# Masked linear gated by a LoRA layer: new orders for the first products and for a build of weights

## Chip, cores and metric

The kernel runs on one core of one Trainium2 chip. The metric is device time in microseconds for one execution. The engines are TensorE (PE in the profile, with PEld for its weight loads), VectorE (DVE), ScalarE (ACT), GpSimd (POOL) and SyncE (SP), which here issues every DMA.

## What is computed

The reference, cut to what matters (x is 2 x 1024 x 1024 in f32, all matrices are 1024 x 1024, the mask is one of 32 x 32 blocks, 8 experts have rank 64):

```python
xn = (x - mean(x)) / sqrt(var(x) + 1e-5)             # over the last axis
bm = mask.reshape(32, 32, 32, 32).sum(axis=(1, 3)) > 0
w  = weight with every 32 x 32 block multiplied by bm
s  = einsum('bsk,nk->bsn', xn, w) + bias
q  = einsum('bi,ki->bk', xn.mean(axis=1), Wq)
coeffs = softmax(einsum('bk,ek->be', q, lora_keys) / sqrt(128))
base  = einsum('bsi,oi->bso', xn, W_org)
h     = einsum('bsi,eir->bser', xn, lora_down)
delta = einsum('be,bser,ero->bso', coeffs, h, lora_up)
out = x + s * silu(base + delta)
```

## The kernel before

**Tiling.** The 2048 rows of x are 16 tiles of 128 rows, two tiles to a group. Groups 0 to 7 multiply all rows by the masked weight (the first matrix, giving s). Groups 8 to 11 and 12 to 15 take the rows of batch 0 and of batch 1 again, now with the second matrix, W_org plus the LoRA part mixed with the batch's coefficients. So the second matrix is built twice, once for each batch; the first build stands between products P58 and P59 (191 to 230 us).

**Products.** PE does all of it in numbered products P0 to P114, most of them four k-chunks of 512 columns (`products()`). f32 operands are split into a high and a low part of type fp32r, and a chunk is three matmuls: high by high, high by low, low by high (lines L1011 to L1013 of `triple`). Groups 0 to 2 are "plain": eight products each, one for every choice of row tile, half of the columns and half of k. P0 to P3 (row tiles 0 and 1, first half of the columns) are not split at all and run as f32 (L1110, `whole`); P4 is row tile 2, P5 row tile 3. From group 3 on, seven products on sums of blocks take the place of eight. Steps E0.c.p are the same kind of product for the first build: part of up by part of down, for column block c and the p-th of the seven.

**What a plain product needs.** A tile of x is loaded (LX), gets its statistics on DVE (SN: L1326 to L1330) and its rstd on POOL (SR), is normalized in two halves (LN: L1335 on DVE, L1552 on POOL), transposed on PE in two halves of four transposes (TX, L1048) and copied out of PSUM by ACT (TC, L1164). The mask comes in four quarters (LM). Each has two counts of 1024 columns (CA: on DVE L1340, on ACT L1198), a compare (CB, DVE, L1347, which writes bmx), a small matmul that spreads it over the partitions (CP, PE, L1040), a copy to SBUF (CM, DVE, L1355) and the multiplications with the weight pieces (W: DVE L1360, POOL L1566). Splits of rows are steps H (ACT, L1221) and V (DVE, L1394); splits of matrices are HB (ACT, L1235) and VB (DVE, L1394); those for the build are U and VU.

**Warm-up.** Before any of it, PE does 29 transposes of an identity matrix (`WARM`, L1030) into an accumulator that nobody reads.

**What sets the order.** Everything is written out by hand. `ORDER` holds five strings, one for each of SP, PE, ACT, DVE and POOL, and each word is one step that the engine takes in that order (`order_of`). Each engine waits on semaphores for what a step needs, so a step that waits holds up all that stand behind it on its engine. SP issues all DMAs in one queue in this way: loads of x (LX, later LT and LG for transposed tiles), masks (LM), weights (LW), keys and Wq (LY, LK), the build's parts of up (LU), of the split down matrix (LD, L943, into b_hi and d_snaps) and of W_org (LE, L958), s and x for the last sums (LB, LR), and stores of xn (RS) and of s (ST). In PSUM there are six accumulators (psA) and two banks for everything small (psM); a step that takes a bank waits until the one before it in that bank has been read.

## Time and profile before

| | us |
|---|---|
| median of the runs shown (429.3, 431.19, 430.07) | 430.07 |
| profiled execution, its own time | 429.73 |
| its span | 427.9 |

| engine | busy us | share of the span |
|---|---|---|
| PE | 414.2 | 97% |
| PEld (weight loads, beside PE) | 336.1 | 79% |
| DVE | 382.6 | 89% |
| ACT | 240.8 | 56% |
| POOL | 52.7 | 12% |

HBM moved 257 GB/s over the span, and the mean granted clock of TensorE was 0.991 of full speed. How to read it: PE's busy times are ends of pipelined matmuls, so that matmuls overlap in the table of busy times, and what PE is doing is read from the distance between two starts. The idle time before an instruction and what ended it stand in brackets in a timeline; engines that are not the bound may idle at no cost. A row of a table of stretches gives the stretch and its length, then the busy time and the number of instructions of each engine (PE, PEld, DVE, ACT, POOL; fewer where the view is cut down to some), then the granted clock as a share of 2.4 GHz, the busy share of the DMA engines and GB/s. Rows that carry the argument stand in a section of their own below.

### The profile page before, as it was taken

The numbers are of one execution on the slowest core, as the hardware profiler recorded it, in microseconds if no ns is written. First come the engines' busy times: TensorE is split into PE (matmuls) and PEld (weight loads), VectorE is DVE, ScalarE is ACT, GpSimd is POOL, SyncE is SP. The second block draws the span as 40 slices with busy tenths as digits, with TensorE's granted clock in tenths as the row PEclk, the third lists the DMA queues.
The fourth block names the chain that finished last, engine by engine and source line by source line (L and its number), as shares of the span: only waits on it lengthen the run. The fifth ranks groups of instructions, "written<-read, shape, count | busy, mean of one in ns | idle before, by whom it ended". The sixth has DMA issues, their size and how long they took to land.

```text
span 427.9 us, 6112 instructions
## 1 busy us (share of the span) xinstructions
PE 414.2 (97%) x1857; PEld 336.1 (79%) x1857; DVE 382.6 (89%) x592; ACT 240.8 (56%) x427; POOL 52.7 (12%) x61
## 2 busy tenths in 40 slices
PE   6699999999999999999999999999999999999995
PEld 6357888888888888877887888887788888888885
DVE  5789989999899999799999989889899999997556
ACT  3385459879835525495457555445754584634412
POOL 4221302321220010000212010100002110001100
PEclk9699999999999999999999999999999999999999
DMA  8994448878688884999997135599899933367674
GB/s 299 408 409 185 125 146 303 312 225 288 221 306 313 300 289 163 364 379 303 295 382 268 61 123 196 170 369 360 295 368 371 352 100 124 94 227 236 189 249 162
DMA packets 45280, 110.51 MB, mean 258 GB/s; under 512 B 4928, under 2 KB 6208, under 8 KB 44480
## 3 DMA queue, kind: packets, MB, share of 16 engines
q1 hardware_dynamic: 45248, 110.12, 73.0%
q8 instruction: 15, 0.25, 0.2%
q14 instruction: 17, 0.14, 0.1%
HBM read 77.60 MB, written 32.51 MB: 257 GB/s over the span
## 4 chain that ended last, share of the span: by engine, by line
PE 36%; DMA 6%; DVE 6%; issue 4%; ACT 2%; SPq 1%; DVEq 0%; ACTq 0%
PE psA L1011 12%; PE psA L1012 12%; PE psA L1013 12%; DMA b_hi<-d_dram 2%; DMA d_snaps<-d_dram 1%; DMA b_raw<-in_up_dram 1%; DMA s_in<-s_dram 1%; DMA xres<-in_x_nat_dram 1%; DVE cst L1509 1%; DVE a_lo L1394 1%; DVE b_lo L1394 1%; DVE b_raw L1404 1%; SPq L974 0%; DVE cst L1477 0%; ACT cst L1295 0%
## 5 line engine op out<-in xcount | busy, mean ns | idle before, releaser
L1011 PE MATMUL psA<-b_hi,a_hi 128*128 128x512 f32 (+1 forms) x444 | 173.4, 391 | 0.6 <-ACT snaps L1279 0.6
L1013 PE MATMUL psA<-b_hi,a_lo 128*128 128x512 f32 (+1 forms) x444 | 172.1, 388 | 0.0
L1012 PE MATMUL psA<-b_lo,a_hi 128*128 128x512 f32 (+1 forms) x444 | 172.0, 387 | 0.0
L1011 PEld LDWEIGHTS psA<-b_hi,a_hi 128*128 128x128 f32 x444 | 83.4, 188 | 18.4 <-ACT snaps L1279 1.3
L1013 PEld LDWEIGHTS psA<-b_hi,a_lo 128*128 128x128 f32 x444 | 83.4, 188 | 17.3
L1012 PEld LDWEIGHTS psA<-b_lo,a_hi 128*128 128x128 f32 x444 | 83.4, 188 | 16.4
L1394 DVE TENSOR_TENSOR b_lo<-b_raw,b_hi 128x512 fp32r<-128x512 f32 (+2 forms) x78 | 59.6, 790 | 0.2 <-ACT b_hi L1235 0.2
L1235 ACT ACTIVATE b_hi<-b_raw 128x512 fp32r<-128x512 f32 (+2 forms) x66 | 44.7, 716 | 20.4 <-DVE b_raw L1401 5.1
L1279 ACT ACTIVATE snaps<-psA 128x512 f32<-128x512 f32 x39 | 23.1, 591 | 39.6 <-PE psA L1013 39.6
L1221 ACT ACTIVATE a_hi<-s_raw 128x512 fp32r<-128x512 f32 x52 | 31.7, 623 | 15.3 <-DVE s_raw L1385 13.6
L1394 DVE TENSOR_TENSOR a_lo<-s_raw,a_hi 128x512 fp32r<-128x512 f32 x52 | 35.1, 689 | 1.0 <-ACT a_hi L1221 0.8
L1221 ACT ACTIVATE a_hi<-xq 128x512 fp32r<-128x512 f32 x43 | 26.2, 622 | 13.4 <-PE psA L1013 8.2
L1394 DVE TENSOR_TENSOR a_lo<-xq,a_hi 128x512 fp32r<-128x512 f32 x43 | 29.2, 686 | 2.5 <-ACT a_hi L1221 2.5
L1509 DVE TENSOR_TENSOR cst<-cst,s_in 128x512 f32<-128x512 f32 x31 | 21.3, 688 | 9.0 <-DMA s_in<-s_dram 4.9
L1477 DVE TENSOR_TENSOR cst<-psA,snaps 128x512 f32<-128x512 f32 x37 | 25.2, 686 | 2.0 <-issue 1.3
L1011 PE MATMUL psA<-b_hi 128*128 128x512 f32 x64 | 25.0, 390 | 0.9 <-DMA b_hi<-d_dram 0.9
L1012 PE MATMUL psA<-b_lo,b_hi 128*128 128x512 f32 x64 | 24.9, 389 | 0.0
L1013 PE MATMUL psA<-b_hi 128*128 128x512 f32 x64 | 24.9, 389 | 0.0
L1515 DVE TENSOR_TENSOR cst<-cst,xres 128x512 f32<-128x512 f32 x30 | 20.5, 688 | 4.7 <-DMA xres<-in_x_nat_dram 4.0
L1295 ACT ACTIVATE cst<-cst 128x512 f32<-128x512 f32 x23 | 14.4, 626 | 13.6 <-DVE cst L1477 12.6
L1374 DVE TENSOR_REDUCE xpart<-xq 128x8 f32<-128x1024 f32 x16 | 19.2, 1212 | 0.0
L1110 PE MATMUL psA<-b_raw,xq 128*128 128x512 f32 x32 | 17.3, 696 | 1.6 <-POOL b_raw L1566 1.6
(143 smaller groups left out, 557.8 us busy)
## 6 DMA issues: line engine op xcount, KB each, us to landing
b_hi<-d_dram SPq DMA_DIRECT2D x24, 512.0 KB, 5.8
xn_dram<-xq SPq DMA_DIRECT2D x16, 512.0 KB, 5.4
s_dram<-cst SPq DMA_DIRECT2D x32, 256.0 KB, 5.2
xq<-xn_dram SPq DMA_DIRECT2D x16, 512.0 KB, 5.2
worg_sb<-in_w_org_dram SPq DMA_DIRECT2D x32, 256.0 KB, 4.9
s_in<-s_dram SPq DMA_DIRECT2D x32, 256.0 KB, 4.2
xres<-in_x_nat_dram SPq DMA_DIRECT2D x32, 256.0 KB, 4.3
out_dram<-cst SPq DMA_DIRECT2D x31, 256.0 KB, 4.0
```

What stands on the lines that cost most here:

```text
L1011: nc.tensor.matmul(ps, l_hi, r_hi, start=first, stop=False, skip_group_check=True)
L1012: nc.tensor.matmul(ps, l_hi, r_lo, start=False, stop=False, skip_group_check=True)
L1013: return nc.tensor.matmul(ps, l_lo, r_hi, start=False, stop=over, skip_group_check=True)
L1110: ins = nc.tensor.matmul(bank, a_quarter(0, i[0], i[2])[:, c * P:(c + 1) * P], w_raw(W_OPS.index(op))[:, c, :], start=c == 0 and first, st ...
L1221: nc.scalar.activation(a_hi[:, m % ARING, :], a_source(m), ACT.Copy).then_inc(act_hi, 1)
L1235: nc.scalar.activation(b_hi[:, hi_of.get(op, op), b_piece(s, op, pc), :], b_source(s, op, pc), ACT.Copy)\
L1279: nc.scalar.activation(snap(n), bank_of(n), ACT.Copy).then_inc(act_post, 1)
L1374: nc.vector.tensor_reduce(xpart[:, t, :], x_tile(t // 2, t % 2).rearrange("p (k r) -> p k r", r=P), AX.X, ALU.add).then_inc(dve_R, 1)
L1394: nc.vector.tensor_tensor(lo, raw, hi.bitcast(F32), ALU.subtract).then_inc(dve_lo, 1)
L1477: nc.vector.tensor_tensor(cst_of(n), bank, snap(copied), ALU.add).then_inc(dve_post, 1)
L1509: nc.vector.tensor_tensor(cst_of(n), cst_of(n), s_in[:, j % 4, :], ALU.mult).then_inc(dve_post, 1)
L1515: nc.vector.tensor_tensor(cst_of(n), cst_of(n), xres[:, j % 4, :], ALU.add).then_inc(dve_res, 1)
```

## The change

Only the table of orders changes, and a new kind of step is added to PE's list. F k.n is n idle transposes of the identity, as in the warm-up, into the same accumulator; PE's list has F0.10 and F1.8 behind the two halves of TX0. The first lines of PE's order, and the new branch:

```diff
-    TX0.0 TX0.1 CP0 P0 TX1.0 TX1.1 CP1 TX2.0 TX2.1 P1 P2 CP2 TX3.0 P3 TX3.1 K P4 CP3 TX4.0 P5 TX4.1 P6 P7 P8 P9 P10
+    CP0 TX0.0 TX0.1 F0.10 F1.8 CP1 TX2.0 TX2.1 P0 TX1.0 TX1.1 P1 P2 CP2 P3 TX3.0 P4 TX3.1 P5 K CP3 P6 TX4.0 P7 TX4.1 P8
...
-                if kind == "CP":
+                if kind == "F":
+                    for _ in range(st[2]):
+                        nc.tensor.matmul(psA[:, ACC - 1, 0:P], ident[:, :], ident[:, :], start=True, stop=True,
+                                         is_transpose=True)
+                elif kind == "CP":
```

The other lists change as follows.

- SP: the second mask and the first two pieces of weights now stand ahead of x 1 and x 3, and the keys and some weights come earlier; the stores of xn and s of the first 60 us are in another order. In the build, two parts of d, two of W_org and three stores change places.
- ACT: begins with three mask counts (one of mask 0, both of mask 1), and takes the second count of mask 3 from DVE; its splits of the first matrix's pieces and its copies of x stand in another order.
- DVE: gives away that count; multiplies weight piece 0 of the first quarter in place of piece 3; compares mask 0 right behind its count. In the build it takes two low splits and a sum in another order.
- POOL: rstd of x 2 ahead of that of x 0, and weight piece 3 in place of piece 0.

The matrices, the tiles and the arithmetic are those of before. In the changed kernel the table of orders is three lines shorter and the new branch adds four, so lines ahead of the branch have a number lower by three (L1011 is L1008, L1030 L1027) and lines behind it one higher by one (L1048 is L1049, L1110 L1111, L1394 L1395).

PE's list from its first step on, before (L1040 is CP, L1048 the transposes of x, L1110 the products P0 to P3; `x_nat_sb` holds tiles 0 and 1, `x_nat` later ones):

```order
L1030 MATMUL psA<-ident 128x128 x29
L1048 MATMUL psA<-ident,x_nat_sb 128x128 x8
L1040 MATMUL psM<-bmx,sel 128x16 x4
L1110 MATMUL psA<-b_raw,xq 128x512 x4
L1048 MATMUL psA<-ident,x_nat_sb 128x128 x8
L1040 MATMUL psM<-bmx,sel 128x16 x4
L1048 MATMUL psM<-ident,x_nat_61 128x128 x8
L1110 MATMUL psA<-b_raw,xq 128x512 x8
```

PE's list now:

```order
L1027 MATMUL psA<-ident 128x128 x29
L1041 MATMUL psM<-bmx,sel 128x16 x4
L1049 MATMUL psA<-ident,x_nat_sb 128x128 x8
L1033 MATMUL psA<-ident 128x128 x18
L1041 MATMUL psM<-bmx,sel 128x16 x4
L1049 MATMUL psM<-ident,x_nat_61 128x128 x8
L1111 MATMUL psA<-b_raw,xq 128x512 x4
L1049 MATMUL psA<-ident,x_nat_sb 128x128 x8
L1111 MATMUL psA<-b_raw,xq 128x512 x8
```

CP0 stands ahead of tile 0's transposes instead of behind them, the 18 idle transposes are new, and CP1 and the transposes of tile 2 moved from behind P0 to ahead of it.

DVE's list behind the statistics of x tiles 0 and 2, before, from mask 0's count (L1340) to the multiplications of the weights (L1360):

```order
L1340 TENSOR_REDUCE cnt<-masks 128x1
L1326 BN_STATS nat_stats<-x_nat_sb 128x6 x2
L1328 BN_AGGR nat_mv<-nat_stats 128x2
L1329 TENSOR_SCALAR stat<-nat_mv 128x1
L1330 TENSOR_SCALAR var<-nat_mv 128x1
L1347 SCALAR_TENSOR_TENSOR bmx<-cnt,diag 128x16
L1355 COPY bmask<-psM 128x64
L1326 BN_STATS nat_stats<-x_nat_61 128x6 x2
L1328 BN_AGGR nat_mv<-nat_stats 128x2
L1329 TENSOR_SCALAR stat<-nat_mv 128x1
L1330 TENSOR_SCALAR var<-nat_mv 128x1
L1360 TENSOR_TENSOR b_raw<-b_raw,bmask 128x512 x3
```

DVE's list at the same place now, from mask 0's count (L1341) on:

```order
L1341 TENSOR_REDUCE cnt<-masks 128x1
L1348 SCALAR_TENSOR_TENSOR bmx<-cnt,diag 128x16
L1336 TENSOR_SCALAR x_nat_sb<-x_nat_sb,stat 128x512
L1356 COPY bmask<-psM 128x64
L1336 TENSOR_SCALAR x_nat_61<-x_nat_61,stat 128x512 x2
L1361 TENSOR_TENSOR b_raw<-b_raw,bmask 128x512 x2
L1348 SCALAR_TENSOR_TENSOR bmx<-cnt,diag 128x16
L1361 TENSOR_TENSOR b_raw<-b_raw,bmask 128x512
L1356 COPY bmask<-psM 128x64
```

The compare (`bmx`) follows the count at once, half of tile 0 is normalized behind it and not ahead of the count, and the statistics of tiles 1 and 3 have moved behind the multiplications.

DVE's list in the first build, where the low splits of up's sums (`a_lo<-a_raw,a_hi`) are made, before, from 190 us on:

```order
L1414 TENSOR_TENSOR b_raw_51<-a_raw_55,b_raw_51 128x512
L1394 TENSOR_TENSOR a_lo_54<-a_raw_55,a_hi_53 128x512 x3
L1394 TENSOR_TENSOR b_lo_50<-b_raw_51,b_hi_49 128x512
L1414 TENSOR_TENSOR temp_62<-a_raw_55,b_raw_51 128x512
L1477 TENSOR_TENSOR cst_60<-psA,snaps_58 128x512
L1394 TENSOR_TENSOR a_lo_54<-a_raw_55,a_hi_53 128x512
L1394 TENSOR_TENSOR b_lo_50<-b_raw_51,b_hi_49 128x512
```

DVE's list at the same place now:

```order
L1415 TENSOR_TENSOR b_raw_51<-a_raw_55,b_raw_51 128x512
L1395 TENSOR_TENSOR a_lo_54<-a_raw_55,a_hi_53 128x512 x3
L1415 TENSOR_TENSOR temp_62<-a_raw_55,b_raw_51 128x512
L1395 TENSOR_TENSOR a_lo_54<-a_raw_55,a_hi_53 128x512
L1395 TENSOR_TENSOR b_lo_50<-b_raw_51,b_hi_49 128x512 x2
L1410 TENSOR_TENSOR b_raw_51<-b_raw_51,worg_sb_67 128x512
L1395 TENSOR_TENSOR a_lo_54<-a_raw_55,a_hi_53 128x512
L1395 TENSOR_TENSOR b_lo_50<-b_raw_51,b_hi_49 128x512
L1478 TENSOR_TENSOR cst_60<-psA,snaps_58 128x512
```

The low split that follows the three in a row stood behind a `b_lo` and a `cst` (the sum for s of block 56) and now stands ahead of both.

SP's list in the first build, from the loads of s at 217.7 us on, before (`d_snaps` is the part of d that the last products of the build take, `worg_sb` is W_org):

```order
L974 DMA s_in_70<-s_dram 128x512 x2
L958 DMA worg_sb_67<-in_w_org_dram 128x512 x4
L915 DMA xn_dram<-xq_56 128x1024
L974 DMA s_in_70<-s_dram 128x512
L943 DMA d_snaps_59<-d7_dram 128x512
L910 DMA xq_56<-xn_dram 128x1024
L958 DMA worg_sb_67<-in_w_org_dram 128x512
```

SP's list around the last load of `d_snaps` now:

```order
L955 DMA worg_sb_67<-in_w_org_dram 128x512
L940 DMA d_snaps_59<-d7_dram 128x512
L955 DMA worg_sb_67<-in_w_org_dram 128x512 x2
L940 DMA d_snaps_59<-d7_dram 128x512
L990 DMA s_dram<-cst_60 128x512
L955 DMA worg_sb_67<-in_w_org_dram 128x512 x2
L990 DMA s_dram<-cst_60 128x512
L907 DMA xq_56<-xn_dram 128x1024
```

The last `d_snaps` stood behind four loads of W_org in a row, a store of xn and loads of s; it now stands ahead of the last two loads of W_org and of those.

## Rows read from the trace of the kernel before

**Rows 1.** The page's first line.

```profile
span 427.9 us, 6112 instructions
```

**Rows 2.** Timeline of PE, first 40 us: start us, us, instruction [idle before <-releaser].

```profile
1.57 5.93 PE L1030 MATMUL psA<-ident 128*128 128x128 f32 x29 [1.57 <-POOL ident L1528]
8.04 1.09 PE L1048 MATMUL psA<-ident,x_nat_sb 128*128 128x128 f32 x8 [0.55 <-DVE x_nat_sb L1335]
...
14.45 6.66 PE L1110 MATMUL psA<-b_raw,xq 128*128 128x512 f32 x8 [1.59 <-POOL b_raw L1566]
...
22.88 7.03 PE L1110 MATMUL psA<-b_raw,xq 128*128 128x512 f32 x16
...
35.98 0.48 PE L1011 MATMUL psA<-b_hi,a_hi 128*128 128x512 f32 x1
```

**Rows 3.** Busy time by engine in stretches, with the granted TensorE clock (PEclk).

```profile
9.20:13.60 4.40, 0.24 (x4) 0.18 (x4) 3.72 (x9) 2.79 (x6) 0.89 (x2) 1.00 1.00 401
13.60:14.40 0.80, 0.00 (x0) 0.00 (x0) 0.77 (x3) 0.00 (x0) 0.80 (x2) 0.53 1.01 420
...
17.10:20.40 3.30, 3.30 (x5) 1.33 (x4) 1.84 (x5) 1.99 (x4) 0.00 (x0) 0.50 1.05 406
...
20.60:23.00 2.40, 2.40 (x23) 2.03 (x22) 0.90 (x3) 0.60 (x1) 0.59 (x1) 1.00 1.03 434
```

**Rows 4.** The same view, the warm-up transposes (L1030) alone.

```profile
1.50:4.20 2.70, 2.63 (x13) 2.63 (x14) 1.00 0.88 311
...
6.80:7.50 0.70, 0.69 (x6) 0.46 (x4) 1.00 0.95 375
```

**Rows 5.** The same view, PE alone, at the end of the span.

```profile
423.60:426.60 3.00, 0.00 (x0) 1.00 0.40 143
426.70:427.80 1.10, 0.00 (x0) 0.50 0.16 53
```

**Rows 6.** Timeline of DVE, 4 to 27 us: a mask count, three mask multiplications.

```profile
9.32 1.22 DVE L1340 TENSOR_REDUCE cnt<-masks 128x1 f32<-128x1024 int32 x1 [1.34 <-DMA masks<-in_mask_dram]
...
14.72 2.07 DVE L1360 TENSOR_TENSOR b_raw<-b_raw,bmask 128x512 f32<-128x512 f32 x3
```

**Rows 7.** Timeline of ACT, 8 to 26 us: copy of x, mask count, split.

```profile
8.73 0.60 ACT L1164 ACTIVATE xq<-psA 128x512 f32<-128x512 f32 x1 [6.67 <-PE psA L1048]
9.32 1.06 ACT L1198 ACTIVATE masks<-masks 128x1024 f32<-128x1024 int32 x1
...
16.23 0.63 ACT L1235 ACTIVATE b_hi<-b_raw 128x512 fp32r<-128x512 f32 x1 [4.24 <-DVE b_raw L1360]
```

**Rows 8.** The first load of weights (line L899): issue and landing.

```profile
L899 SPq DMA_DIRECT2D b_raw<-in_weight_dram x1: 446/446/446, 3.1 to 3.1; - x1
...
DMA to landing us min/median/max: 10.0/10.0/10.0
```

**Rows 9.** Timeline of PE in the first build, two places.

```profile
194.26 0.39 PE L1012 MATMUL psA<-a_lo,b_hi 128*128 128x512 f32 x1
194.48 0.39 PE L1013 MATMUL psA<-a_hi,b_hi 128*128 128x512 f32 x1
195.09 0.50 PE L1011 MATMUL psA<-a_hi,b_hi 128*128 128x512 f32 x1 [0.22 <-DVE a_lo L1394]
195.43 0.40 PE L1012 MATMUL psA<-a_lo,b_hi 128*128 128x512 f32 x1
...
228.35 0.39 PE L1013 MATMUL psA<-a_hi,d_snaps 128*128 128x512 f32 x1
228.96 0.47 PE L1011 MATMUL psA<-a_hi,d_snaps 128*128 128x512 f32 x1 [0.22 <-DMA d_snaps<-d_dram]
```

**Rows 10.** Timeline of DVE in the first build.

```profile
194.35 0.69 DVE L1394 TENSOR_TENSOR a_lo<-a_raw,a_hi 128x512 fp32r<-128x512 f32 x1
```

**Rows 11.** Timeline of SyncE in the first build: DMA issues.

```profile
218.58 3.55 SPq L958 DMA_DIRECT2D worg_sb<-in_w_org_dram  x4
...
223.26 1.27 SPq L943 DMA_DIRECT2D d_snaps<-d_dram  x1
```

143 lines of the change are left out of this document (70 added, 73 removed).

## The prediction

> **What bounds the kernel now.** I read the page first, then the timeline of TensorE (PE) over the first 40 us with the granted clock beside it, then every place after that where PE's next matmul starts late. The profiled execution took 429.73 us by its own time, 1.83 us more than its span of 427.9 us [rows 1]; the median of the runs shown is 430.07 us. PE is the bound: a 512-column matmul of the split products starts 0.22 to 0.23 us after the one ahead of it [rows 9] from 36 us on, and only a few starts come late. So time can be won in two places only: before PE runs without pause, and at those late starts.
>
> At the start, PE works off 29 warm-up transposes and the eight transposes of x tile 0, ends them at 9.13 us and then has 0.24 us of work up to 14.45 us, when the first product (P0) can begin [rows 2, 3]. P0 takes 6.66 us for its four matmuls of full-width f32 (each leaves two records), 1.67 us each, while the eight of P1 and P2 take 7.03 us, 0.88 us each [rows 2]. The granted clock says why: 1.00 up to 13.6 us, 0.50 (the 1.2 GHz level) from there on while P0 runs, and 1.00 (2.4 GHz) again after 20.5 us [rows 3]. So the clock fell 4.5 us after the last real work and rose 6.0 us after PE took up work for good at 14.45 us. At the half rate P0 lost 6.66 - 3.52 = 3.1 us. The same fall stands at the end of the trace: PE is idle from 423.6 us, and at 426.7 us the clock reads 0.50 [rows 5]. The warm-up shows the rise: 13 transposes in 2.63 us (0.20 us each) at first, six in 0.69 us (0.115 us each) after 6.8 us [rows 4], 5.2 us after PE began at 1.57 us.
>
> **The start, step by step.** Both orders load the same bytes ahead of the first piece of weights: 512 KB of x twice, 1 MB of mask, then 1 MB (two x tiles before, the second mask now). So mask 0 is counted from 9.32 us on [rows 6] and the weights land at 3.1 + 10.0 = 13.1 us [rows 8], as before. What moves is behind the count. VectorE (DVE) counts until 10.54 us and now makes bmx at once, where two statistics steps on x tile 1 stood between; mask 0's CP0 thus runs at about 11.0 us, not 12.6. DVE then normalizes half of tile 0 and PE takes its eight transposes (TX0) at about 11.4 us, not 8.04. DVE masks the two weight pieces as they land, 0.69 us each [rows 6], until 14.4 us; P0's first piece is no longer GpSimd's. ScalarE has now two counts of mask 1 (1.06 us each), one split of b (0.63) and then the copy of x (0.60) ahead of P0 [rows 7], from 11.9 us: ready at 15.0 us. PE has the 18 idle transposes behind TX0, and CP1 and the eight of tile 2 (1.1 us) ahead of P0. P0's start is thus set by PE, and by its clock:
>
> (a) Clock at 1.00 throughout: TX0 11.4 to 12.3; 18 x 0.107 = 1.9 us of idle transposes to 14.3; CP1 at 14.6, since bmx of mask 1 stands behind the weight piece; TX2 to 15.7; P0 15.8 to 19.3; TX1 and ScalarE's copy 1.4 us; P1 at 20.7 us against 22.88 us [rows 2]: -2.2 us. (0.107 us is the spacing at the full clock, the 0.115 of [rows 4] less its last tail.)
>
> (b) Clock falls before TX0. PE now has nothing but CP0 from 7.5 to 11.4 us: 3.9 us, against 5.3 us in which it did fall, and 3.1 us at the end of the trace after which it had fallen. From 11.4 us on PE runs without pause, so I let the clock rise 5.2 to 6.0 us later, the two delays read above: at 16.6 to 17.4 us. Work from TX0 to the end of P0 is 0.9 + 1.9 + 0.1 + 0.9 + 3.5 = 7.3 us at the full clock, and half of the 5.2 to 6.0 us is lost: P0 ends at 21.3 to 21.7, P1 starts at 22.7 to 23.1 us: -0.2 to +0.2 us.
>
> (c) Clock falls at 13.6 us as before, behind 12 of the idle transposes. The other six take 1.2 us, to 14.8; CP1 and TX2 at half rate to 16.6; P0 mostly at the full clock to 20.2 to 20.5; P1 at 21.6 to 21.9 us: -1.0 to -1.3 us.
>
> I take the middle of (b) and (c), -0.6 us: the pause after the warm-up is nearer to those in which the clock fell than to the 0.55 us before TX0 in which it did not [rows 2], while the steady run begins 3.0 us earlier.
>
> The page "TensorE: Matmul & The Clock Gate" of the Trainium skill, Part 4 (PE-mode transpose), speaks against the idle transposes: it says that transposes do not count as a busy PE and that the full clock does not engage for them. By it the sum would be that of the second rival below. The trace disagrees: the spacing fell from 0.20 to 0.115 us when PE had run nothing but transposes.
>
> **What is late behind that.** P1 to P15 follow without gap as before: SyncE's loads of x 1 and 3 come later by 1 MB but land at 15.6 and 18.4 us, before their statistics; the second half of the mask work (W1) ends on DVE at 24.8 us and P2's third matmul needs it at 26 us or later. DVE and ScalarE have the same work, with one count of 1.2 us moved to ScalarE, so the splits ahead of P4 to P8 move with PE; the nearest, x tile 3's low half for P5, has about 1 us. GpSimd's move (rstd of tile 2 ahead of tile 0) delays LN0.1 to 9.6 us, still before DVE's half. Moving the transposes and the keys' products between the products costs two more changes from a full-width f32 run to a split one: the first matmul behind each takes 0.48 us instead of 0.39 [rows 2, 9], so +0.2 us. Each late step here would cost what it is late, at most some 0.7 us (one DVE pass).
>
> **The build, step by step.** Two late starts fall to the new orders. At 194.48 us the next matmul of E0.0.2 starts 0.61 us later, not 0.23, and the one after 0.34 us later: 0.5 us lost, ended by DVE's low part of u [rows 9]. That pass ended at 195.04 us [rows 10]. The new order takes two passes of 0.69 us, issued every 0.60 us, from ahead of it (a split for chain product 5 and the sum of block 56): 1.2 us earlier, 0.7 us before PE wants it. The two are late next: the split is then done at about 198 us and PE wants it at 199.5; the sum moves by some 5 us, and no bank that PE takes before 200 us hangs on it, as far as I can follow. The matmul after the one of 228.35 us again starts 0.61 us later, 0.38 us lost, this time for the last piece of d [rows 9]: its load was issued at 223.26 us, behind four loads of W_org that were let go one by one from 218.58 us, and took 1.27 us to issue [rows 11]. It now stands ahead of the last two of them, of a store of x and of a load of s; its own condition (a product at about 209 us) is long met. I take 0.3 us of 0.38, since the accumulator behind it has little to spare. The wait for the gate at 185 us is untouched. Sum: -0.8 us; bounds -0.9 (both gone) and 0 (both stay).
>
> Nothing after absorbs this: later waits hang on PE's own progress.
>
> **Sum.** -0.6 + 0.2 - 0.8 = -1.2 us on 429.73: 428.5; I give 428.6 us, since the profiled execution lies 0.3 us under the median. Own range of this case: from -1.3 + 0.1 - 0.9 to +0.2 + 0.2 - 0.6, so 427.6 to 429.6 us, with 0.3 us for the median 427.6 to 429.9 us.
>
> **Rivals.** First, the clock never falls, case (a): -2.2 + 0.2 - 0.8 = -2.8, so 426.9 us. For it: PE has 0.7 us of warm-up after 6.8 us, and the 1.09 us of TX0 at 8.04 us was enough company for it before. Against it: 3.9 us with nothing but four 16-column matmuls.
>
> Second, on the slower side: transposes do not hold or raise the clock. Then it falls in the pause, TX0 takes 1.7 us, the idle transposes 18 x 0.204 = 3.7 us to 16.8 us, TX2 1.7; P0 starts at 18.7 us and, with 6.0 us to the rise, ends at 25.2; P1 at 26.5 us: +3.6. With +0.2 and -0.8: 432.7 us. It decides as soon as the clock rises later than 24 us. Against it stands the warm-up [rows 4].
>
> Third, the orders do not do what they say: the clock rises at 20.5 us again, so that P1 starts at 23.6 to 24.2 us (+0.7 to +1.3), and another pass is late in the build in place of the two: 430.1 to 431.0 us.
>
> **Chances.** Forecast 0.50, first rival 0.33, second 0.06, third 0.11. A measurement of this kernel tells about 0.5% (2.15 us) from no change: below 427.9 us is faster, above 432.2 slower. Faster: 0.31 of the first rival and 0.07 of the forecast's lower end, 0.38. Slower: nearly all of the second, 0.05. Within: 0.57. The range reaches from the first rival, 0.3 us below its time, to the lower end of the third: 426.6 to 430.2 us.
>
> **What will show it.** In the new trace: CP0 near 11.0 us and TX0 near 11.4; the granted clock between 10 and 20 us and P0's four matmuls (3.5 us at the full clock, 6.7 at half); P1 between 21.6 and 23.1 us (20.7 by the first rival, 26 by the second); starts every 0.23 us in E0.0.2 and in E0.3.3, where 0.61 us stood twice. The prediction is wrong if P1 comes earlier than 21 us or later than 23.5, or if PE waits for a split of b or a between P4 and P16.

## The result: slower by one per cent

| | before | after |
|---|---|---|
| median of five runs each, us | 430.07 (429.02 to 431.19) | 434.62 (434.06 to 436.43) |
| ratio, with its 95% interval | | 1.0105 [1.0076, 1.0135] |
| profiled execution, its own time, us | 429.73 | 435.68 |

The change costs about 4.5 us. The prediction said 428.6 us, 426.6 to 430.2, and gave "slower" a chance of 0.05: it was wrong in size and in sign. The profiled execution of after is one of the longer ones, so that its losses add up to some 6 us, not 4.5. The clock falls once more in its build: the mean granted clock is 0.987, as in one other of the five, and the three at 0.990 to 0.994 have spans of 432.3 to 432.9 us, 1 to 2 us shorter. That fall is not shown to be what makes them shorter: from 226 to 260 us PE loses as much in traces in which the clock stays up (see the end of the section on the build).

The page of the profile after, first line and four of its engines (busy us, share of the span, instructions), beside [rows 1] and the table of the profile before:

```profile
span 434.0 us, 6149 instructions
PE 419.0 (97%) x1875; PEld 340.3 (78%) x1875; DVE 391.0 (90%) x591; ACT 242.3 (56%) x429; POOL 61.6 (14%) x61
```

DVE is busy 391.0 us where it was 382.6, and POOL 61.6 where it was 52.7, though DVE gave one count of a mask to ACT and POOL has the same number of passes of the same size. Passes on these two engines have become longer. That line of the page is the whole case in small.

Where PE gained and lost can be read by setting the same matmul of both traces side by side. Start in after less start in before, worked out from the two timelines of PE (minus is earlier):

| matmul, at its time before | after less before, us |
|---|---|
| P1, 22.88 us | -0.60 |
| P15, 68.30 us | +1.28 |
| 191.08 us | +1.59 |
| E0.0.2, 195.09 us | +1.20 |
| E0.3.3, 227.22 us (its first) | +3.04 |
| P59, 230.42 us | +4.24 |
| 259.91 us | +4.91 |
| 296.71 us | +5.16 |
| the last, 420.32 us | +6.08 |

P1 came when it was predicted. Behind it stand two losses that the prediction did not have: 1.9 us between P1 and 68 us, and 3.3 us between 191 and 260 us, across the first build. The last 1.2 us come after 260 us.

### The start

PE after, from the start (start us, us, instruction and count, in brackets the idle time before and what ended it). It answers to [rows 2]:

```profile
1.57 5.54 PE L1027 MATMUL psA<-ident 128*128 128x128 f32 x29 [1.57 <-POOL ident L1529]
...
9.85 0.26 PE L1041 MATMUL psM<-bmx,sel 128*128 128x16 bf16 x4 [2.73 <-DVE bmx L1348]
10.21 1.97 PE L1049 MATMUL psA<-ident,x_nat_sb 128*128 128x128 f32 x8
11.97 4.05 PE L1033 MATMUL psA<-ident 128*128 128x128 f32 x18
...
17.02 3.60 PE L1111 MATMUL psA<-b_raw,xq 128*128 128x512 f32 x8
...
21.78 0.66 PE L1049 MATMUL psA<-ident,x_nat_sb 128*128 128x128 f32 x4 [0.73 <-DVE x_nat_sb L1336]
22.27 7.20 PE L1111 MATMUL psA<-b_raw,xq 128*128 128x512 f32 x16
...
48.29 0.47 PE L1008 MATMUL psA<-b_hi,a_hi 128*128 128x512 f32 x1 [0.44 <-DVE b_lo L1395]
...
60.50 0.66 PE L1049 MATMUL psM<-ident,x_nat_sb 128*128 128x128 f32 x4 [0.60 <-ACT xq L1165]
```

Busy time in three stretches of it (PE, PEld, DVE, ACT, POOL, then the granted clock), which answers to [rows 3]:

```profile
7.20:9.40 2.20, 0.00 (x0) 0.00 (x0) 1.51 (x4) 1.15 (x2) 1.66 (x3) 1.00 1.02 428
9.60:15.80 6.20, 5.84 (x30) 5.74 (x31) 3.66 (x9) 3.30 (x6) 1.58 (x1) 0.50 1.00 369
16.50:17.00 0.50, 0.50 (x7) 0.50 (x6) 0.50 (x2) 0.00 (x0) 0.00 (x0) 1.00 1.07 434
```

PE has nothing to do from 7.11 to 9.85 us and the granted clock falls to 0.50 (1.2 GHz) at 9.45. PE then works without pause, on transposes nearly alone, and the clock is back at 1.00 (2.4 GHz) from 16.28 us. The 18 idle transposes go by at some 0.2 us each, and P0 takes 3.60 us where it took 6.66. Three small late starts are new in the rows above: 0.73 us for x tile 1's normalization ahead of P1, and 0.44 and 0.60 us at 48 and 60 us. The one at 48.29 us is for a low split of b, one of the prediction's own signs of being wrong. DVE shows why (same columns):

```profile
8.20 1.22 DVE L1341 TENSOR_REDUCE cnt<-masks 128x1 f32<-128x1024 int32 x1 [0.65 <-DMA masks<-in_mask_dram]
...
19.46 2.27 DVE L1336 TENSOR_SCALAR x_nat_sb<-x_nat_sb,stat 128x512 f32<-128x512 f32 x1
...
42.18 3.76 DVE L1395 TENSOR_TENSOR a_lo<-xq,a_hi 128x512 fp32r<-128x512 f32 x1
```

And POOL beside it:

```profile
18.80 0.77 POOL L1553 TENSOR_SCALAR x_nat_sb<-x_nat_sb,stat 128x512 f32<-128x512 f32 x1
19.53 1.91 POOL L1567 TENSOR_TENSOR b_raw<-b_raw,bmask 128x1024 f32<-128x1024 f32 x1
...
41.74 3.65 POOL L1567 TENSOR_TENSOR b_raw<-b_raw,bmask 128x2048 f32<-128x2048 f32 x1 [13.30 <-DVE bmask L1356]
```

The normalization of 512 columns takes 0.55 us elsewhere and 2.27 here; the low split takes 0.69 us elsewhere and 3.76 here. Both run beside a multiplication on GpSimd, and both end shortly after it: 21.73 against 21.44 us, 45.94 against 45.39. The split began 0.44 us after the multiplication. The normalization began 0.07 us ahead of it, while GpSimd was still at its own normalization of 0.77 us; which of the two GpSimd passes caught it, no run separates. In the runs below that have the same start, what is caught near 20 us is now this normalization and now a low split (2.39 us in the start alone).

### The build

PE after at the last product of the build, E0.3.3, where [rows 9] has 0.61 us between two starts:

```profile
228.03 0.39 PE L1010 MATMUL psA<-b_hi 128*128 128x512 f32 x1
230.25 0.50 PE L1008 MATMUL psA<-a_hi,d_snaps 128*128 128x512 f32 x1 [1.83 <-DVE b_raw L1405]
```

The two waits that the new orders were predicted to shorten are gone: E0.0.2 no longer waits for its low split, and `d_snaps` no longer ends a wait. But E0.3.3 waits 1.83 us for a sum on DVE that is to free its accumulator. What DVE does ahead of that sum:

```profile
222.12 1.57 DVE L1381 TENSOR_TENSOR b_raw<-b_raw 128x512 f32<-128x512 f32 x1
...
225.42 2.98 DVE L1395 TENSOR_TENSOR b_lo<-b_raw,b_hi 128x512 fp32r<-128x512 f32 x3
...
229.52 0.68 DVE L1405 TENSOR_TENSOR b_raw<-psA,b_raw 128x512 f32<-128x512 f32 x1
```

And POOL:

```profile
221.31 1.83 POOL L1592 TENSOR_TENSOR b_raw<-b_raw 128x512 f32<-128x512 f32 x1 [7.89 <-DVE b_lo L1395]
226.48 1.36 POOL L1577 TENSOR_TENSOR b_raw<-b_raw,worg_sb 128x512 f32<-128x512 f32 x1 [3.34 <-ACT b_raw L1265]
```

A pass of 0.68 us, begun at 222.12 while GpSimd's runs until 223.14, ends at 223.69. Three splits take 2.98 us instead of 1.89, and the longest of them (1.77 us) ends at 228.39, again 0.55 us after GpSimd's 227.84. Four such meetings stand between 208 and 228 us, 0.57 + 0.49 + 0.88 + 1.09 = 3.0 us; before had two, at 207 and 213 us, about 1.0 us in all. The difference, 2.0 us, is as large as the step at E0.3.3: the matmul ahead of it starts 1.04 us later than in before, E0.3.3 itself 3.04. So far this is a match of size; the run with GpSimd's build passes made short, below, tests it.

The kernel before has the same GpSimd pass at the same place, and it costs DVE nothing. POOL before:

```profile
225.44 1.30 POOL L1576 TENSOR_TENSOR b_raw<-b_raw,worg_sb 128x512 f32<-128x512 f32 x1 [6.09 <-ACT b_raw L1264]
```

DVE before, beside it:

```profile
225.47 0.68 DVE L1404 TENSOR_TENSOR b_raw<-psA,b_raw 128x512 f32<-128x512 f32 x1
226.07 0.68 DVE L1401 TENSOR_TENSOR b_raw<-psA,worg_sb 128x512 f32<-128x512 f32 x1
226.67 0.68 DVE L1394 TENSOR_TENSOR b_lo<-b_raw,b_hi 128x512 fp32r<-128x512 f32 x1
```

Two passes that read one operand from PSUM (`psA`) run beside GpSimd at their usual 0.68 us; the split, which reads two from SBUF, begins within 0.1 us of GpSimd's end (226.74) and is not held either. In all of after nine DVE passes are stretched by more than 0.2 us, by 10.8 us in sum; in before two, by 1.0 us.

DVE's list changed more here than the description of the change says (it names two low splits and a sum). Of some 95 steps that DVE takes in the build, about half stand elsewhere, and steps of ACT and SP move too; only GpSimd's list is that of before.

Last, the clock, in two stretches around that wait (all engines as above):

```profile
228.50:230.20 1.70, 0.00 (x0) 0.00 (x0) 1.70 (x4) 0.00 (x0) 0.00 (x0) 1.00 0.96 220
...
231.40:234.60 3.20, 3.20 (x9) 2.48 (x8) 3.20 (x6) 0.63 (x1) 0.68 (x1) 0.50 0.31 113
```

After the 1.8 us without a matmul the granted clock reads 0.50 from 231.3 to 234.7 us. Matmuls start 0.43 us apart there where 0.23 is the rule, 1.6 us more up to P59 in this execution; less the 0.38 us of `d_snaps` that were won, this carries +3.04 us to +4.24.

These 1.6 us are no loss on top of the wait. Two traces have this fall, after and the run without idle transposes; from 226 to 260 us PE loses 3.87 and 3.82 us in them. Three more have the new build and the same wait of 1.8 us with the clock up (the build alone, the mask passes made short, the start mended), and there PE loses 3.85, 3.88 and 3.85 us. With the clock up PE comes sooner to low splits that are late as well, and waits for them. The kernel with the mask passes made short, PE some 8 us behind E0.3.3, and a stretch of PE around it:

```profile
236.98 0.50 PE L1011 MATMUL psA<-b_hi,a_hi 128*128 128x512 f32 x1 [0.53 <-DVE b_lo L1398]
```

```profile
231.50:237.50 6.00, 5.47 (x24) 1.00 0.36 94
```

### The profile page after: what moved, and what is told of

Same layout as the page of the kernel before. It is cut to its first block and busy times, and to the rows that moved or that the text cites. A ratio compares the mean times of both kernels' runs of the same rounds, so it can differ in the third digit from the quotient of the medians.

```text
span 434.0 us, 6149 instructions
## 1 busy us (share of the span) xinstructions
PE 419.0 (97%) x1875; PEld 340.3 (78%) x1875; DVE 391.0 (90%) x591; ACT 242.3 (56%) x429; POOL 61.6 (14%) x61
## 5 line engine op out<-in xcount | busy, mean ns | idle before, releaser
L1008 PE MATMUL psA<-b_hi,a_hi 128*128 128x512 f32 (+1 forms) x444 | 173.7, 391 | 2.0 <-ACT snaps L1280 1.0
L1008 PEld LDWEIGHTS psA<-b_hi,a_hi 128*128 128x128 f32 x444 | 83.5, 188 | 20.5 <-ACT snaps L1280 1.9
L1395 DVE TENSOR_TENSOR b_lo<-b_raw,b_hi 128x512 fp32r<-128x512 f32 (+1 forms) x78 | 62.2, 818 | 0.1
L1395 DVE TENSOR_TENSOR a_lo<-s_raw,a_hi 128x512 fp32r<-128x512 f32 x52 | 35.0, 685 | 0.7 <-ACT a_hi L1222 0.5
L1395 DVE TENSOR_TENSOR a_lo<-xq,a_hi 128x512 fp32r<-128x512 f32 x43 | 33.1, 773 | 2.8 <-ACT a_hi L1222 2.8
L1510 DVE TENSOR_TENSOR cst<-cst,s_in 128x512 f32<-128x512 f32 x31 | 22.3, 721 | 6.3 <-DMA s_in<-s_dram 3.6
L1008 PE MATMUL psA<-b_hi 128*128 128x512 f32 x64 | 25.2, 394 | 0.9 <-DMA b_hi<-d_dram 0.8
L1296 ACT ACTIVATE cst<-cst 128x512 f32<-128x512 f32 x23 | 14.4, 626 | 16.8 <-DVE cst L1478 15.8
L1386 DVE TENSOR_TENSOR s_raw<-xq 128x512 f32<-128x512 f32 x23 | 15.5, 684 | 5.3 <-DMA xq<-xn_dram 2.9
```

The costliest lines, as they stand in the source:

```text
L1008: nc.tensor.matmul(ps, l_hi, r_hi, start=first, stop=False, skip_group_check=True)
L1386: nc.vector.tensor_tensor(s_raw[:, j - 1, :], a, b, op).then_inc(dve_S, 1)
L1395: nc.vector.tensor_tensor(lo, raw, hi.bitcast(F32), ALU.subtract).then_inc(dve_lo, 1)
L1510: nc.vector.tensor_tensor(cst_of(n), cst_of(n), s_in[:, j % 4, :], ALU.mult).then_inc(dve_post, 1)
```

## The experiments

**Theory A**: a DVE pass with two inputs from SBUF (and the normalization) that starts while GpSimd runs a pass is held until GpSimd's has ended; the new orders put such passes beside GpSimd's, which makes the late starts. **Rivals**: the orders as such hang DVE's work badly, meetings or not (B in the expectations); the new start only shifts the old build into a worse phase; the idle transposes cost what they give. Ratios are to the kernel before, run on the same chip with it (its median there: 429.9 to 431.0 us).

| run | median us (runs) | ratio [95%] |
|---|---|---|
| e1_start_alone | 433.73 (8) | 1.0083 [1.0054, 1.0112] |
| e2_build_alone | 433.01 (12) | 1.0049 [1.0029, 1.0069] |
| e3_build_cut | 432.06 (12) | 1.0035 [1.0010, 1.0060] |
| e4_before_idle | 431.74 (12) | 1.0017 [0.9991, 1.0042] |
| e5_no_idle | 436.01 (6) | 1.0123 [1.0087, 1.0159] |
| e6_masks_cut | 433.60 (11) | 1.0066 [1.0040, 1.0093] |
| e7_idle_sp | 429.80 (12) | 0.9986 [0.9959, 1.0013] |
| e8_idle_sp_dve | 430.33 (12) | 1.0005 [0.9981, 1.0028] |
| e9_both_cut | 428.18 (12) | 0.9949 [0.9923, 0.9976] |
| e10_before_pool | 433.67 (9) | 1.0075 [1.0044, 1.0106] |
| e11_build_dve | 435.39 (6) | 1.0118 [1.0080, 1.0156] |
| e12_start_mended | 433.40 (12) | 1.0074 [1.0052, 1.0096] |

### Half of the change: the start, the build

The start alone takes the new orders up to product P29 and leaves the rest as before; the build alone the other way round. Of the differences, DVE's list in the build, as the start alone has it against after:

```diff
-    UT0.4.1 VU0.2.1 VU0.6.1 VU0.6.0 EG0.0.0
+    VU0.5.0 UT0.4.1 QC56 VU0.2.1 VU0.6.0 EG0.0.0
```

> The new orders up to product 29 with the old orders behind it (first build as before). Theory A (VectorE's passes with two SBUF inputs wait for GpSimd's passes where the two meet, and the new orders let them meet: 10.8 us of stretched VectorE passes in the trace of after against 1.0 in before): the meetings at 19.5 and 42.2 us stay, since the start is the same, PE is some 1.3 to 1.7 us late at 180 us, and the old build runs as in before: 431.3 to 432.0 us. Theory B (the start's later phase is what upsets the build, whichever order the build has): the build loses 2 us or more again: 433.5 to 435 us.

> The old orders up to product 29 with the new orders behind it. Theory A: the new order in the build lets VectorE's low splits meet GpSimd's passes at about 222 and 227 us whatever came ahead, so PE waits some 2 us in E0.3.3, and gains 0.5 us at E0.0.2: 432 to 433.5 us. Theory B (phase of the start): without the late start VectorE is early enough, both late starts of before are gone and nothing new is late: 429.0 to 429.6 us.

The build alone: 433.01 us, ratio 1.0049. E0.0.2 starts in time, DVE passes are stretched at the same five places (205.8, 210.6, 219.9, 224.4 and 232.1 us), and E0.3.3 waits 1.83 us for the same sum, with all of the old start in front. So the loss belongs to the build's own orders. The start alone: 433.73 us, more than A expected. At 195 us PE is 0.63 us behind before; in after it is 1.20, but there the clock was low for 6.8 us at the start and here for 3.4. Then the *old* build loses too: a sum at 226.87 us takes 1.55 us beside GpSimd's pass, and E0.3.3 waits 1.17 us for it. The rival of the phase is right here: the old build was free of meetings that PE pays for only at the time at which it ran. The two halves come to a little more than the whole (0.83% and 0.49% against 1.05%). Both pay at E0.3.3 for the same kind of meeting, but a difference of this size lies within the intervals.

### GpSimd's build passes made short

Five of GpSimd's passes in the first build, in after's orders, cut to one column or to a fill with zeros:

```diff
-                    nc.gpsimd.tensor_tensor(o, a, b, op).then_inc(pool_T, 1)
+                    if s == 1 and j == 1:
+                        nc.gpsimd.memset(o, 0.0).then_inc(pool_T, 1)
+                    else:
+                        w = slice(0, 1 if s == 1 else H)
+                        nc.gpsimd.tensor_tensor(o[:, :, w], a[:, :, w], b[:, :, w], op).then_inc(pool_T, 1)
```

> The changed kernel with GpSimd's passes of the first build taken out as far as they go: the sums EG0.1.3, EG0.3.3 and T1.0.4 work on one column of 512, T1.0.1 and T1.2.1 are a fill with zeros, so the second matrix of batch 0 is wrong in these parts. VectorE's order is untouched. Theory A: VectorE's passes of 1.2 to 1.8 us in the build go back to 0.68, PE's wait of 2.2 us at 228 us falls under 0.4 us, and the clock doesn't fall behind it: 431 to 432.5 us against 434.6. Theory B (the new VectorE order itself puts the sum that PE waits for too late): the wait stays at 1.5 us or more: 434 us.

DVE of this kernel, the same three splits:

```profile
224.19 1.89 DVE L1398 TENSOR_TENSOR b_lo<-b_raw,b_hi 128x512 fp32r<-128x512 f32 x3
```

And PE at E0.3.3:

```profile
228.24 0.39 PE L1013 MATMUL psA<-b_hi 128*128 128x512 f32 x1
228.46 0.39 PE L1011 MATMUL psA<-a_hi,d_snaps 128*128 128x512 f32 x1
```

The three splits take 1.89 us, E0.3.3 starts 0.22 us after the one ahead of it, the clock stays up, and between 195 and 230 us PE *gains* 0.6 us on the kernel before (+1.41 to +0.77) where after lost 3.0. Counted from 191 us, with the late start of E0.0.2, it gains 1.0 us (+1.79 to +0.77); the prediction had 0.8. With the passes short, the new build does what was predicted of it. One doubt is left: GpSimd's results also come sooner here. The run with added GpSimd passes, below, has no such doubt.

### GpSimd's mask passes made short

The same for two mask multiplications at the start (W1.0 at 19.5 us, W3.0 at 41.7 us), cut to their first 32 columns:

```diff
                     tile, factor = w_operands(q, pc)
+                    if (q, pc) in ((1, 0), (3, 0)):
+                        tile, factor = tile[:, 0:1, :], factor[:, 0:1, :]
                     nc.gpsimd.tensor_tensor(tile, tile, factor, ALU.mult).then_inc(pool_w, 1)
```

> The changed kernel with GpSimd's two long multiplications of the mask (W1.0, W3.0) cut to the first 32 columns of each row, so that these parts of the weight stay unmasked and s is wrong. Theory A (VectorE's passes wait for them): the normalization of 2.27 us at 19.5 us goes back to 0.54 and the split of 3.76 us at 42.2 us to 0.68, PE's waits of 0.7 us ahead of P1 and of 0.6 and 0.77 us at 47.6 and 59.6 us go, and the splits of the second matrix begin 2 us ahead of after. In time that gives 432.5 to 433.7 us if the build passes it on, and no more than 0.5 us off after if the build takes it back as it did with the start of e4. Rival (the waits come from the order, not from the meetings): PE's waits stay, 434.5 us.

DVE of this kernel, the normalization and the low split that took 2.27 and 3.76 us:

```profile
20.00 0.54 DVE L1339 TENSOR_SCALAR x_nat_sb<-x_nat_sb,stat 128x512 f32<-128x512 f32 x1
...
42.05 0.68 DVE L1398 TENSOR_TENSOR a_lo<-xq,a_hi 128x512 fp32r<-128x512 f32 x1
```

The waits at 48 and 60 us are gone. Between P1 and 68 us PE now loses nothing against before (0.59 us ahead at P1, 0.61 at 68 us), and nothing in the run with both cuts either (1.15 and 1.17 us). The five traces with the new start and these passes whole (after, the start alone, the build passes made short, no idle transposes, the passes given to VectorE) lose 1.8 to 2.8 us there: the loss behind P1 is these two meetings. At 195 us PE is 0.38 us ahead of before instead of 1.20 behind. The build, left as it is, loses its 3.3 us from 191 to 260 us as in after.

Both cuts together:

> The changed kernel with both cuts of e3 and e6: GpSimd's two long mask multiplications and its five passes of the first build are cut to a stub or a fill, so s and the second matrix of batch 0 are wrong in these parts. If the meetings of VectorE with GpSimd account for what after lost (3.0 us by e3 and 1.7 us by e6 against a loss of 4.5), nothing is left: PE stands 1 to 1.5 us ahead of before at 240 us, and the time is that of before within 1 us (ratio 0.997 to 1.003). If the orders lose time on their own, it stays over 1.004.

428.18 us, ratio 0.9949: faster than before by 2.2 us by the ratio, more than was expected of it; PE is 1.4 us ahead at 195 us, 2.1 at 230 and 1.5 at the end. This is near the time that was predicted for the orders (428.6 us), reached once the meetings are taken out, but that it is so near is in part chance: the ratio says -2.2 us where the prediction had -1.5, and in the profiled execution the clock was low for only 3.4 us at the start. It is no kernel to use, as it leaves work out.

### Nothing taken away: GpSimd passes added to the kernel before

Six idle multiplications of 256 columns on GpSimd, behind T1.0.4 in the kernel before; nobody reads their result and nothing else moves:

```diff
-... T1.0.4 EG0.3.3 ...
+... T1.0.4 Z6 EG0.3.3 ...
+                elif kind == "Z":
+                    idle = bmask[:, :, :]
+                    for _ in range(st[1]):
+                        mine(nc.gpsimd.tensor_tensor(idle, idle, idle, ALU.mult))
```

> The kernel before with nothing moved, and six idle GpSimd passes (256 columns, both inputs from SBUF, 0.6 to 0.8 us each, their result read by nobody) behind T1.0.4 in the first build, at about 219.4 us. VectorE runs splits and sums with two SBUF inputs there until 225 us. Theory A: each of those passes that starts while one of the six runs is held until its end, VectorE falls 2 to 4 us behind, E0.3.3 starts 1 to 3 us late: 432 to 434 us against 430.6. Rival (GpSimd's passes do not hold VectorE; the long passes in after are something else): every pass stays at 0.68 us and the time is that of before.

POOL of this kernel, the six passes:

```profile
220.54 6.86 POOL L1595 TENSOR_TENSOR bmask<-bmask 128x256 f32<-128x256 f32 x6
```

DVE beside it and just ahead of it:

```profile
219.34 1.28 DVE L1404 TENSOR_TENSOR b_raw<-psA,b_raw 128x512 f32<-128x512 f32 x2
...
221.74 1.10 DVE L1380 TENSOR_TENSOR b_raw<-b_raw 128x512 f32<-128x512 f32 x1
...
223.78 3.14 DVE L1394 TENSOR_TENSOR b_lo<-b_raw,b_hi 128x512 fp32r<-128x512 f32 x3
```

PE at E0.3.3:

```profile
230.88 0.50 PE L1011 MATMUL psA<-a_hi,d_snaps 128*128 128x512 f32 x1 [2.36 <-DVE b_raw L1404]
```

DVE's passes with two SBUF inputs now take 1.10 us and follow each other every 1.02 us, one for each GpSimd pass, where 0.60 us is the rule; the two at 219.34 us, which read PSUM beside the GpSimd pass of 219.29 us, take 1.28 us together, 0.68 us each as always. E0.3.3 waits 2.36 us: PE, 1.15 us behind before just ahead of it, is 3.67 us behind at it. The kernel is slower by 0.75%, with DVE's list, PE's list and all loads untouched. This shows theory A by addition, and it shows that the price of the change in the build can be had without the change.

The Trainium skill states the rule: page "SBUF — State Buffer", section "Who interferes with whom", says that GpSimd's SBUF ports are shared with VectorE's second pair, that a VectorE instruction with two SBUF inputs contends with a GpSimd instruction that reads SBUF, that `tensor_scalar` can in its two-port modes, that one with at most one SBUF input does not outside such modes, and that the one that issues first holds the ports for the whole instruction. The rows above agree: 3.76 us for a split and 2.27 for a normalization beside GpSimd, 0.68 beside it with an operand in PSUM. The order of issue agrees for the split (42.18 us, after GpSimd's 41.74). The normalization began 0.07 us ahead of the multiplication and was held all the same, with GpSimd's pass before that still running; that row does not test the order.

### GpSimd's build passes given to VectorE

If the meetings cost 3 us, the five passes could go to DVE, which does them in 0.69 us each:

```diff
-... S7.2 EG0.1.3 T1.0.1 T1.0.4 EG0.3.3 T1.2.1 S9.2 ...
+... S7.2 S9.2 ...
```

> The changed kernel with GpSimd's five passes of the first build given to VectorE, each behind the step that it needs; nothing is left out. VectorE gets 5 x 0.6 = 3.0 us more work and loses 4.1 us of waiting in the build (0.57 + 0.49 + 0.88 + 1.09 + 1.09). Theory A: PE's wait of 2.0 us in E0.3.3 shrinks to 1.0 to 1.6 us, and the time is 0.5 to 1.5 us under after: ratio to before 1.006 to 1.010. Rival (the work given to VectorE weighs as much as the waiting did or more): 1.010 to 1.014.

435.39 us: no gain. DVE's passes are all 0.69 us, but five more of them before the sum that E0.3.3 waits for are as late as the meetings were, and the wait is 1.67 us. Here the rival won: what counts is DVE's total ahead of that sum, and 3 us of work weighs about as much as 3 us of being held.

### The start's DVE order mended

Five steps of DVE's list move against after: the normalization (LN1.1) goes ahead of a split, so that two statistics steps (SN3, SN4) stand beside GpSimd's W1.0, and the statistics of tile 5 and a sum over one operand (R1) stand beside W3.0 where the split V4 stood:

```diff
-    V2 V0 LN1.1 VB0.0.2 SN3 VB0.0.1 SN4 W1.1
+    V2 LN1.1 V0 SN3 SN4 VB0.0.2 VB0.0.1 W1.1
...
-    R1 VB0.1.1 KD CM3 QC2 V4 VB0.7.0 V8 SN5
+    VB0.1.1 KD CM3 QC2 SN5 R1 V4 VB0.7.0 V8
```

> The changed kernel, nothing left out, with five steps of VectorE's list moved so that passes with one SBUF input stand beside GpSimd's two long multiplications: the normalization LN1.1 goes ahead of the split V0 and the statistics SN3 behind it (ahead: W1.0 at 19.5 us), and SN5 and R1 (1.3 + 0.5 + 1.2 us) go ahead of V4 (W3.0 at 41.7 us). Theory A: LN1.1 takes 0.54 us instead of 2.27 and P1 starts 0.7 us earlier (21.5 us); V4 is held for under 1 us instead of 3.1, VectorE gains some 3 us of work by 46 us, and of PE's waits at 47.6 and 59.6 us (0.6 and 0.77) at least one goes: PE stands 0 to 0.7 us behind before at 70 us instead of 1.3. In time, against after, -0.5 to -1.5 us (ratio to before 1.007 to 1.010), since the build is that of after. Rival: the waits move with the order and PE at 70 us stays 1.3 us behind.

POOL of this kernel, its long multiplication, then DVE, the two passes once more and, between them, statistics that stand beside that multiplication:

```profile
40.98 3.65 POOL L1570 TENSOR_TENSOR b_raw<-b_raw,bmask 128x2048 f32<-128x2048 f32 x1 [16.14 <-DVE bmask L1359]
```

```profile
18.72 0.55 DVE L1339 TENSOR_SCALAR x_nat_sb<-x_nat_sb,stat 128x512 f32<-128x512 f32 x1
...
41.41 1.27 DVE L1330 BATCH_NORM_STATS2 nat_stats<-x_nat_sb 128x6 f32<-128x512 f32 x2
...
44.23 0.95 DVE L1398 TENSOR_TENSOR a_lo<-xq,a_hi 128x512 fp32r<-128x512 f32 x1
```

P1 starts at 21.64 us, the wait at 60 us is gone, and between P1 and 68 us PE loses 0.7 us instead of 1.8 to 2.8, with all of the work done. The statistics beside GpSimd's pass take their usual time. At 195 us PE is 0.62 us ahead of before, 1.8 us better than after; some of that is the clock, low for 3.4 us at the start here and for 6.8 in after. Against the two traces with after's start and 3.4 us of low clock (0.63 us behind before in the start alone, 0.99 in the passes given to VectorE) it is 1.2 to 1.6 us. The build keeps its loss. The median, 433.40 us, is 1.2 us below after's, but the two intervals overlap, so only the trace tells the gain.

### The idle transposes

After without them, and the kernel before with 30 of them behind its TX0 and 14 behind its CP0:

```diff
-    CP0 TX0.0 TX0.1 F0.10 F1.8 CP1 TX2.0 TX2.1 P0
+    CP0 TX0.0 TX0.1 CP1 TX2.0 TX2.1 P0
```

```diff
-    TX0.0 TX0.1 CP0 P0 TX1.0
+    TX0.0 TX0.1 F0.30 CP0 F1.14 P0 TX1.0
```

> The changed kernel without its 18 idle transposes. In the trace of after the clock had fallen at 9.5 us, before the first of them, and they ran at 0.2 us each until 15.8 us; the clock rose at 16.3. Theory 1 (they keep PE at work, so that the clock is back when P0 starts): without them the clock rises 3 us or more later, P0 takes 5 us or more in place of 3.6, P1 starts no earlier than 22.3 us: 434.5 to 436 us. Theory 2 (they only stand in the way of P0): P0 starts at 14.5 to 15.5 us and P1 1 us earlier: 433.5 us.

> The kernel before with idle transposes alone: 30 behind the transposes of x tile 0 and 14 behind CP0, where PE had nothing to do from 9.1 to 14.4 us. If idle transposes hold the clock: 1.00 throughout the start, P0 takes 3.5 us in place of 6.66, P1 starts 2 to 3 us earlier unless the next loads or VectorE are late: 427 to 428.5 us. If they do not (the rule of the notes): the clock falls near 13.6 us or earlier, the transposes themselves take 0.2 us each, and P0 starts later: 430.5 to 433 us.

Without them in after, the clock stays at 0.50 for 10.2 us instead of 6.8, P0 takes 5.70 us and P1 starts at 23.75 us against 22.27: by these two traces they are worth 1.5 us there. The seven traces with the idle transposes in the new start have the clock low for 3.4 or 6.8 us and P1 at 20.67 to 22.28 us, so the sign holds, though only one trace is without them. The times (1.0123 against 1.0105) are too close to tell. In the kernel before, PE:

```profile
8.99 3.44 PE L1036 MATMUL psA<-ident 128*128 128x128 f32 x30
...
12.65 1.73 PE L1036 MATMUL psA<-ident 128*128 128x128 f32 x14
...
14.72 3.70 PE L1114 MATMUL psA<-b_raw,xq 128*128 128x512 f32 x8 [0.35 <-POOL b_raw L1570]
...
20.81 3.60 PE L1114 MATMUL psA<-b_raw,xq 128*128 128x512 f32 x8
```

And the stretch at whose start the clock fell in before [rows 3]:

```profile
13.60:17.10 3.50, 3.15 (x14) 1.57 (x12) 3.43 (x9) 0.63 (x1) 2.24 (x2) 1.00 1.00 418
```

The clock holds 1.00 throughout, with nothing but transposes and one mask step on PE from 9 to 14.4 us; P0 takes 3.70 us and P1 comes 2.07 us earlier. All 12 executions have a mean granted clock of 0.994 to 1.000, those of before on the same chip 0.985 to 0.992. This is the first rival of the prediction (the clock never falls, -2.2 us), made by filling the pause and not by shortening it. And yet the median is 431.74 us, no gain. The lead is still -1.78 us at 220 us and then goes, first on DVE:

```profile
223.29 0.69 DVE L1413 TENSOR_TENSOR temp<-temp,worg_sb 128x512 f32<-128x512 f32 x1 [1.50 <-DMA worg_sb<-in_w_org_dram]
223.90 1.79 DVE L1413 TENSOR_TENSOR b_raw<-b_raw,worg_sb 128x512 f32<-128x512 f32 x1
```

then on PE:

```profile
226.95 0.50 PE L1011 MATMUL psA<-a_hi,d_snaps 128*128 128x512 f32 x1 [1.20 <-DVE b_raw L1408]
```

The load of W_org comes at its old time, DVE waits 1.50 us for it, and the pass behind it now falls beside GpSimd's.

### Making room for that lead

On top of the kernel before with idle transposes, SyncE loads W_org and the last `d_snaps` ahead of s:

```diff
-    LD0.2.2 LB0 LB2 LE0.3.3 LE0.3.1 LE0.2.3 LE0.2.2 RS15 LB3 LD0.3.3 LG10.0
+    LD0.2.2 LE0.3.3 LE0.3.1 LE0.2.3 LD0.3.3 LB0 LB2 LE0.2.2 RS15 LB3 LG10.0
```

and in a second one DVE also takes its passes around E0.0.2 in a better order:

```diff
-    VU0.5.0 UT0.4.1 QC56 VU0.2.1 VU0.6.0
+    UT0.4.1 VU0.2.1 VU0.5.0 QC56 VU0.6.0
```

> e4 (the kernel before with 44 idle transposes) with one more move in SyncE's list in the first build: three loads of W_org and the last load of d go ahead of the two loads of s, which wait from 211.4 to 216.9 us for the store of s ahead of them to land. In e4 VectorE waited 1.5 us for W_org at 221.8 us, and then a sum of 0.69 us took 1.79 beside a GpSimd pass. Theory: that queue is what took the start's gain back; with W_org there in time both go, E0.3.3 starts without the 1.36 us wait, and PE stays 1.6 to 2 us ahead of before at 240 us: 428.5 to 429.5 us against before at 430.9. Rival (something behind, at 296 to 335 us, takes it back anyway): 430.5 us or more.

> e7 with the changed kernel's move on VectorE in the build that mends the late start of E0.0.2: a low split (VU0.5.0) and the sum of block 56 go behind the low split VU0.2.1. Expected: the wait of 0.35 to 0.4 us at 193 us goes, 0.4 us less than e7, unless the later sum makes a new wait before 200 us, which would show as a late start there.

The first carries its lead through the build as expected, with no wait at E0.3.3 and -1.73 us at 230 us. Its median of 429.80 us is 0.75 us below before, inside the interval. Later loads take the lead back; DVE at 274 us:

```profile
274.54 1.29 DVE L1513 TENSOR_TENSOR cst<-cst,s_in 128x512 f32<-128x512 f32 x2 [2.73 <-DMA s_in<-s_dram]
```

It waits another 1.77 us for W_org at 325 us, in the second build. (The profiled execution, 431.76 us, is 2 us above the median, so that its loss at the end is larger than that of most.) The second, with DVE reordered too, removes the wait at 193 us and gets another of 0.42 us at 196 us, for a low split that moved back: 430.33 us, no gain. No complete kernel beat the kernel before by more than can be measured.

## Why the prediction failed

**Right, with some luck: the start up to P1.** P1 was predicted at 21.6 to 23.1 us and came at 22.27. Other executions of the same start put it elsewhere: 20.67 us in the start alone and 21.09 in the passes given to VectorE, where the clock was low for 3.4 us and not 6.8. These lie near the first rival's 20.7 us, and the first of them is under the 21 us that the prediction named as a sign of being wrong. The clock fell in the pause after the warm-up, as case (b) said, and P0 ran at full clock (3.60 us). A small miss lies within it: the first mask was said to be counted from 9.32 us "as before" and was counted from 8.20, so the pause was 1.1 us shorter and P0 began at 17.02 us, 0.8 us ahead of case (b) (whose end of 21.3 us less 3.5 is 17.8). That is the execution and not the order, since with the same loads the count begins between 8.2 and 9.6 us in the traces of the new start. The held normalization took some 0.5 us of it back: from P0 to P1 it is 5.25 us in after and 4.72 with the mask passes short. Transposes raised and held the clock: the second rival (432.7 us) falls by the rows at 9.60 to 15.80 us and by the kernel before with 44 of them. With it falls, for these runs, the rule weighed there: the Trainium skill, page "TensorE: Matmul & The Clock Gate", Part 4 (PE-mode transpose), says that transposes do not engage the full clock; here the clock rose, and was held, with next to nothing else on PE.

**Wrong: "P1 to P15 follow without gap as before".** The step counted DVE's passes, found the same number, and let a late one cost 0.7 us "at most". The order of the passes also settles what runs beside GpSimd. In before GpSimd's 1024-column mask pass ran beside statistics and splits of an operand in PSUM (22.41 to 24.32 us) and the 2048-column one beside statistics and sums over one operand (40.78 to 44.44 us, the next split starting at 44.56); in after the one meets a normalization and the other a split. Priced at +0.2 us (two changes of matmul type), the stretch from P1 to 68 us cost 1.9, and 1.8 to 2.8 us in the five traces with this start. With the two GpSimd passes short it costs 0.0, and with five steps of DVE's list moved 0.7.

**Right, then undone: the build's -0.8 us.** Both late starts went as said: the low split of E0.0.2 and the `d_snaps` load end no wait any more, and with GpSimd's passes short the build gains 0.6 to 1.0 us. But the term needed a second half. "The new order takes two passes of 0.69 us [...] from ahead of it" followed two of DVE's steps where about half of its list in the build moved, and put everything else at nothing, those two because they are wanted later and the others without a reason; GpSimd's list, which the change leaves alone in the build, was not looked at. In place of -0.8 us the stretch from 191 to 260 us cost +3.3 us in all five traces with the new build and GpSimd's passes whole (3.28 to 3.34). E0.3.3 waits 1.83 us for a sum that stands behind held passes, and low splits held at about 234 and 250 us make the rest, or the clock does where it falls. The third rival had the kind of it, "another pass late in the build in place of the two", with about 1 us and a chance of 0.11; it had no mechanism, so it had no size.

**Wrong: "nothing after absorbs this".** It did not matter to the sign here, but the kernel before with idle transposes shows it: 2.07 us won at P1 and 1.78 still there at 220 us are gone at the end, after waits for loads of W_org and s that SyncE issues at their old time and a meeting behind one of them; the shares were not separated. A gain at the start of this kernel lasts until the next load that is only just early enough. By this the forecast's -0.6 us at the start may not have been worth 0.6 at the end; with the meetings taken out, the run with both cuts kept its lead.

**What the sum should have been.** By the table of starts: -0.6 us at P1, +1.9 to 68 us, +0.3 to 191 us, -0.5 for E0.0.2, then +3.9 from 226 to 260 us (2.0 of it at E0.3.3), which with rounding gives the +4.9 at 260 us; +1.2 more come up to the end. This is the profiled execution, with 6.1 us in all. The part behind 260 us differs from trace to trace (-1.0 to +1.8 us in the eight that have the new orders in the build, with GpSimd's passes whole, short or moved), with waits for loads and for ACT between 297 and 340 us. How the 4.5 us of the medians divide over these stretches stays open.

Three slips of the sum itself changed nothing in the outcome: it adds 0.1 of the 0.34 us between profile and median, its range takes -0.6 for the build's worse bound where the step gave 0, and the third rival's 430.1 us lies under its own terms (429.73 + 0.7).

## What to carry to other kernels

When an order of VectorE's work is changed, draw GpSimd's passes beside it, even those that the change leaves alone: a two-input SBUF pass that starts under a GpSimd pass costs about the rest of that pass, and here a normalization with one SBUF input was held too, while statistics, sums over one operand and passes with an operand in PSUM ran beside it at no cost, so put those there. A hand-made order that has few such meetings is in tune with its own times, and any shift ahead of it, an earlier start included, can bring the meetings in. A gain at the head of a pipeline is worth what the tightest load behind it leaves of it.
